# Attention values of one unit in four fed to TensorE in float32, and the splits of the rest moved to ScalarE and GpSimd

## The reference

```
x = x + 0.5 * ffn(layernorm(x))        # shared SwiGLU of width 704, plus top 2 of 8 experts of width 352
x = x + attention(layernorm(x))        # 16 query heads, 4 key/value heads, head size 32, rotary, no mask
x = x + 0.5 * ffn(layernorm(x))        # the same weights again
```

## Time and profile before

| | us |
|---|---|
| median of 3 runs | 1815.87 (1813.20 to 1818.67) |
| profiled execution | 1809.72 |
| its span | 1807.7 |
| TensorE busy | 1684.5 (93%) |
| VectorE busy | 1078.8 (60%) |
| ScalarE busy | 864.4 (48%) |
| GpSimd busy | 974.3 (54%) |
| mean granted clock of TensorE | 0.974 |

### The profile page before, as it was taken

How to read it: one execution, slowest core, us unless ns; L and a number is a source line. 1 busy time by engine, 2 the same in 40 slices (tenths; PEclk the granted TensorE clock), 3 DMA queues, 4 the chain that set the end, 5 groups by cost and what they waited for, 6 DMA issues and landing times.

```text
span 1807.7 us, 25091 instructions
## 1 busy us (share of the span) xinstructions
PE 1684.5 (93%) x8596; PEld 1344.3 (74%) x8596; DVE 1078.8 (60%) x1846; ACT 864.4 (48%) x1274; POOL 974.3 (54%) x727
## 2 busy tenths in 40 slices
PE   6999999999977989999999999877799999999997
PEld 5888898999866756666666666545688889999985
DVE  4554322222687879999999999995445432222226
ACT  4322232322324359999999998872323122322320
POOL 3115673336522148989898988840030619550745
PEclk9999999999988989999999999998989999999999
DMA  9205543333630000000000000003010535432427
GB/s 333 97 24 218 207 175 131 120 132 120 193 134 1 1 2 1 1 2 1 1 1 2 1 1 2 13 13 142 1 53 1 222 122 196 161 140 84 167 86 240
DMA packets 54310, 160.01 MB, mean 89 GB/s; under 512 B 6704, under 2 KB 7600, under 8 KB 51632
## 3 DMA queue, kind: packets, MB, share of 16 engines
q1 hardware_dynamic: 41360, 84.74, 13.3%
q0 software_dynamic: 12832, 73.67, 11.4%
HBM read 102.29 MB, written 55.84 MB: 87 GB/s over the span
## 4 chain that ended last, share of the span: by engine, by line
PE 60%; DVE 15%; ACT 12%; issue 6%; DMA 6%; POOL 1%; SPq 0%; ACTq 0%; POOLq 0%; DVEq 0%
PE PS L1021 11%; PE PS L1023 10%; PE PS L1022 10%; ACT PT L1487 5%; DVE nmf L1799 4%; PE PS L1217 4%; DMA xn<-x_routed 3%; ACT Ph L1494 3%; DMA xs<-x_routed 2%; PE PS L1143 2%; PE PS L1148 2%; PE PS L1146 2%; PE PS L1145 2%; PE PS L1147 2%; PE PS L1144 2%
## 5 line engine op out<-in xcount | busy, mean ns | idle before, releaser
L1956 POOL TENSOR_TENSOR Pl<-PT,Ph 128x1024 fp32r<-128x1024 f32 x176 | 433.4, 2475 | 86.4 <-ACT Ph L1494 81.4
L1799 DVE TENSOR_REDUCE nmf<-PS 128x1 f32<-128x1024 f32 x256 | 307.8, 1213 | 30.6 <-PE PS L1217 30.4
L1487 ACT ACTIVATE PT<-PS 128x1024 f32<-128x1024 f32 x256 | 259.5, 1014 | 23.7 <-PE PS L1235 17.0
L1250 PE MATMUL PS<-Ph,V 128*65 128x512 f32 x512 | 205.5, 401 | 13.5 <-DVE Pl L1822 12.7
L1494 ACT ACTIVATE Ph<-PT 128x1024 fp32r<-128x1024 f32 x184 | 194.9, 1059 | 35.0 <-PE PS L1251 32.6
L1251 PE MATMUL PS<-Pl,V 128*65 128x512 f32 x512 | 202.1, 395 | 0.0
L1871 POOL TENSOR_TENSOR W<-raw,W 128x544 fp32r<-128x544 f32 x144 | 190.1, 1355 | 1.5
L1217 PE MATMUL PS<-KS,QS 96*128 96x512 f32 x512 | 171.5, 416 | 19.0 <-ACT PT L1487 13.2
L1774 DVE TENSOR_TENSOR thid<-thid,PS 128x352 f32<-128x352 f32 x78 | 40.7, 521 | 245.8 <-ACT thid L1413 245.8
L1235 PE MATMUL PS<-QS,KS 98*128 98x512 f32 x512 | 173.2, 420 | 3.0 <-DVE nmf L1799 2.9
L1413 ACT ACTIVATE thid<-PS 128x352 f32<-128x352 f32 x78 | 36.2, 464 | 260.4 <-PE PS L1148 260.4
(11 more groups left out here) (183 smaller groups left out, 4107.9 us busy)
## 6 DMA issues: line engine op xcount, KB each, us to landing
raw<-ffn_w POOLq DMA_DIRECT2D x18, 2176.0 KB, 10.2
y_routed<-ytile SPq DMA_DIRECT2D x78, 256.0 KB, 2.1
xn<-x_routed SPq DMA_DIRECT2D x40, 256.0 KB, 2.8
x_routed<-xq SPq DMA_DIRECT2D x1, 9984.0 KB, 28.5
xs<-x_routed SPq DMA_DIRECT2D x38, 256.0 KB, 4.0
raw<-ffn_w SPq DMA_DIRECT2D x6, 768.0 KB, 10.6
raw<-ffn_w SPq DMA_DIRECT2D x2, 2176.0 KB, 9.2
x_home<-X SPq DMA_DIRECT2D x4, 1024.0 KB, 5.8
```

The lines of the kernel that those rows point to most:

```text
L1250: e.matmul(PS[0:VCOL, ob, :], V[:, b * QT + kt, g, :], Ph[:, u % PBUF, js], start=kt == 0, stop=False)
L1487: e.activation(PT[:, u % PTBUF, :], PS[:, i:i + 2, :].rearrange("p b n -> p (b n)"), ACT.Exp, scale=SCALE).then_inc(p_ready.sem, 1)
L1799: e.tensor_reduce(nmf[:, (n % 3) * REP + h, t:t + 1], PS[:, i:i + 2, :].rearrange("p b n -> p (b n)"), AX.X, ALU.max, negate=True).then_in ...
L1956: e.tensor_tensor(Pl[:, u % PBUF, :], PT[:, u % PTBUF, :], Ph[:, u % PBUF, :], ALU.subtract).then_inc(pl_pool.sem, 1)
```

## The change

- Units for which in_full(u) holds (u % 4 == 3, but not u % 16 == 15 outside group 7) are not split. Their values are two matmuls of V and PT, both read as plain float32, FULL_LAG = 3 units after their scores.
- All other units are split with Ph on ScalarE and Pl on GpSimd; only in group 7 does VectorE make Pl, for u % 4 == 1. VectorE makes no Ph.
- LAG is 5. Where the unit whose values are due is not the first of its half head and a next group exists, its values are issued in two halves: one key tile between scores and row_max, one behind row_max.
- A full unit's values come before the third unit's, so a half head ends with unit 2 of four where unit 3 is full (ends_half), else with unit 3.
- The copy to OT moves from ScalarE to VectorE, as does the copy of turned queries for the groups from 2 on.
- Buffers: 4 of PT, 6 of Ph, 5 of Pl, some of them in the place that Wo, MT, rL and head had; Wo and woraw move, and the first Wo load waits for the values of group 3.
- At the end of the loop, the values still due are issued as the split ones, then the full unit 255, then 254.

```diff
-PTBUF = 4
-PBUF = 4
-LAG = 4
+PTBUF, PHBUF, PLBUF = 4, 6, 5
+LAG, FULL_LAG = 5, 3
...
-def hi_on_vector(u):
-    return u % 4 == 1 or u // UNITS == len(KV_GROUPS) - 1 and u % 4 == 3
+def in_full(u):
+
+    return u % 4 == 3 and (u // UNITS == len(KV_GROUPS) - 1 or u % 16 != 15)
 
 
 def lo_on_vector(u):
-    return u % 4 == 2 or u // UNITS == len(KV_GROUPS) - 1 and u % 4 != 0
+    return u // UNITS == len(KV_GROUPS) - 1 and u % 4 == 1
+
+
+def ends_half(u):
+
+    return in_full(u + 1) if u % 4 == 2 else u % 4 == 3 and not in_full(u)
...
         work.append(("scores", u))
-        in_flight.append(u)
         if lows:
             work.append(("place_low", *lows.pop(0)))
+        w = u - LAG if u >= LAG and not in_full(u - LAG) else None
+
+        between = w is not None and unit(w)[3] > 0 and n + 1 < groups
+        if between:
+            work.append(("half_values", w, 0))
         if n + 1 < groups:
             work.append(("row_max", n + 1, un // QT, un % QT))
...
+        if w is not None:
+            work.append(("half_values", w, 1) if between else ("values", w))
+            if ends_half(w):
                 outputs.append(unit(w)[:3])
+        if u >= FULL_LAG and in_full(u - FULL_LAG):
+            work.append(("values", u - FULL_LAG))
...
+    end = groups * UNITS
+    assert in_full(end - 1) and LAG > FULL_LAG
+    for w in [v for v in range(end - LAG, end - 2) if not in_full(v)] + [end - 1, end - 2]:
         work.append(("values", w))
...
                 if c == 0:
+
                     sp.wait_ge(q_done, PROJECTED[-1])
-                    sp.wait_ge(max_turned, 0, REP - 1)
+                    sp.wait_ge(pv_done, NKV * UNITS - 1)
...
+            for j in tiles:
                 kt = 2 * pair + j
                 js = slice(j * GRP, (j + 1) * GRP)
-                e.matmul(PS[0:VCOL, ob, :], V[:, b * QT + kt, g, :], Ph[:, u % PBUF, js], start=kt == 0, stop=False)
-                mm = e.matmul(PS[0:VCOL, ob, :], V[:, b * QT + kt, g, :], Pl[:, u % PBUF, js],
-                              start=False, stop=kt == QT - 1)
-            mm.then_inc(pv_done.sem, 1)
-            free[ob] = (ot_ready, n, h, hf)
+                end = ends_half(u) and j == 1
+                if in_full(u):
+                    mm = e.matmul(PS[0:VCOL, ob, :], V[:, b * QT + kt, g, :].bitcast(F32), PT[:, u % PTBUF, js],
+                                  start=False, stop=end)
+                else:
+                    e.matmul(PS[0:VCOL, ob, :], V[:, b * QT + kt, g, :], high_part(u)[:, js],
+                             start=kt == 0, stop=False)
+                    mm = e.matmul(PS[0:VCOL, ob, :], V[:, b * QT + kt, g, :], low_part(u)[:, js],
+                                  start=False, stop=end)
+            if 1 in tiles:
+                mm.then_inc(pv_done.sem, 1)
+                free[ob] = (ot_ready, n, h, hf)
...
-                if u >= PTBUF:
-                    act.wait_ge(pl_dve if lo_on_vector(u - PTBUF) else pl_pool, u - PTBUF)
+                if u >= PTBUF and in_full(u - PTBUF):
+                    act.wait_ge(pv_done, u - PTBUF)
+                elif u >= PTBUF:
+                    parts_ready(act, u - PTBUF)
...
+            elif kind in VALUES and is_whole(key) and ends_half(key[0]):
...
+                dve.wait_ge(pv_done, u)
+                if i >= 1:
+                    dve.wait_ge(ot_turned, *heads[i - 1])
+                e.tensor_copy(OT[0:VCOL, :], PS[0:VCOL, out_bank(n, hf), :]).then_inc(ot_ready.sem, 1)
+            elif kind == "turn" and beside_heads(key[0]):
+                n, t = key
+                dve.wait_ge(stack_turned, n, t)
+                e.tensor_copy(QS[n % 3][0:STK, :, t * P:(t + 1) * P],
+                              PS[0:STK, MISC, :].rearrange("p (h n) -> p h n", n=P)).then_inc(stack_ready.sem, 1)
```

More of the change, by code:

```diff
@@ L412, in order_of_work @@
             maxima.append((n + 1, un // QT))
[L413 to L418, removed]
+        if in_parts and lo_on_vector(u - 1):
+            work.append(("split_lo", u - 1))
+        if w is not None:
+            work.append(("half_values", w, 1) if between else ("values", w))
+            if ends_half(w):
                 outputs.append(unit(w)[:3])
+        if u >= FULL_LAG and in_full(u - FULL_LAG):
+            work.append(("values", u - FULL_LAG))
         if outputs and pair == 1:
@@ L428, in order_of_work @@
             work.append(("wo", un // QT))
[L429 to L432, removed]
+    end = groups * UNITS
+    assert in_full(end - 1) and LAG > FULL_LAG
+    for w in [v for v in range(end - LAG, end - 2) if not in_full(v)] + [end - 1, end - 2]:
         work.append(("values", w))
-        if unit(w)[3] == QT // 2 - 1:
-            outputs.append(unit(w)[:3])
+        if outputs:
+            work.append(("store_head", *outputs.pop(0)))
+    outputs.append(unit(end - 2)[:3])
     work.append(("store_head", *outputs.pop(0)))
@@ L584, in macaron @@
     assert at <= g_at[LATE] + group_bytes
-    MT, at = place("MT", (QT, 2, 2, P), F32, wqkv_at)
+    assert ORDER[0] * TPG // QT == 1
+    Wo, at = place("Wo", (P, 2, DC, D), F32R, wqkv_at - NT // 2 * NKV * VCOL * 4)
+    woraw, _ = place("woraw", (P, D), F32, arena + NT * D * 4 + NKV * S * 4)
+    MT, at = place("MT", (QT, 2, 2, P), F32, at)
     rL, at = place("rL", (P, 2, TPG), F32, at)
     head, at = place("head", (P, 2, TPG, HD), F32, at)
-    Wo, at = place("Wo", (P, 2, DC, D), F32R, at)
-    woraw, at = place("woraw", (P, D), F32, at)
+    parts_at = [x_at + i * 2 * GRP * 4 for i in range(8)]
+    while len(parts_at) < PHBUF + PLBUF:
+        parts_at.append(at)
+        at += 2 * GRP * 4
     assert at <= wqkv_at + 2 * DC * QKV * 4
+    parts = [place(f"Ph{i}", (P, 2 * GRP), F32R, parts_at[i])[0] for i in range(PHBUF)]
+    parts += [place(f"Pl{i}", (P, 2 * GRP), F32R, parts_at[PHBUF + i])[0] for i in range(PLBUF)]
     PS = ctx.enter_context(nc.psum_tensor("PS", [P, 8, GRP], F32))
@@ L814, in macaron @@
         elif kind == "split_hi":
-            (ph_dve if hi_on_vector(*key) else ph_act).plan(*key)
+            ph_act.plan(*key)
         elif kind == "split_lo":
             (pl_dve if lo_on_vector(*key) else pl_pool).plan(*key)
[L818 to L821, removed]
+        elif kind in VALUES and is_whole(key):
+            u = key[0]
+            pv_done.plan(u)
+            if ends_half(u):
+                ot_ready.plan(*unit(u)[:3])
         elif kind == "store_head":
@@ L878, in is_projected_after, with parts_ready, high_part, low_part @@
         return PROJECTED.index(t) >= n
+    def parts_ready(lane, u):
+        if in_full(u):
+            lane.wait_ge(p_ready, u)
+        else:
+            lane.wait_ge(pl_dve if lo_on_vector(u) else pl_pool, u)
+    def high_part(u):
+        return parts[u % PHBUF]
+    def low_part(u):
+        return parts[PHBUF + u % PLBUF]
     def turned_halves(t):
@@ L893, in macaron @@
     head_place = {key: i for i, key in enumerate(heads)}
-    ends = [tuple(unit(key[0])[:3]) for kind, *key in work if kind == "values" and unit(key[0])[3] == QT // 2 - 1]
+    ends = [tuple(unit(key[0])[:3]) for kind, *key in work
+            if kind in VALUES and is_whole(key) and ends_half(key[0])]
     end_place = {key: i for i, key in enumerate(ends)}
@@ L1238, in scores, with values @@
             free[i] = free[i + 1] = (p_ready, u)
-        def values(u):
+        def values(u, *tiles):
             n, h, hf, pair = unit(u)
@@ L1327, in tensor_program @@
             elif kind == "values":
+                values(*key, 0, 1)
+            elif kind == "half_values":
                 values(*key)
@@ L1461, in scalar_program @@
                              src.unsqueeze(2).broadcast_to([P, REP, 2, HD]), ACT.Copy).then_inc(stack_hi.sem, 1)
-            elif kind == "turn":
+            elif kind == "turn" and not beside_heads(key[0]):
                 n, t = key
@@ L1484, in scalar_program @@
                 act.wait_ge(s_done, u)
-                if u >= PTBUF:
-                    act.wait_ge(pl_dve if lo_on_vector(u - PTBUF) else pl_pool, u - PTBUF)
+                if u >= PTBUF and in_full(u - PTBUF):
+                    act.wait_ge(pv_done, u - PTBUF)
+                elif u >= PTBUF:
+                    parts_ready(act, u - PTBUF)
                 e.activation(PT[:, u % PTBUF, :], PS[:, i:i + 2, :].rearrange("p b n -> p (b n)"),
                              ACT.Exp, scale=SCALE).then_inc(p_ready.sem, 1)
-            elif kind == "split_hi" and not hi_on_vector(*key):
+            elif kind == "split_hi":
                 u, = key
                 act.wait_ge(p_ready, u)
[L1492 to L1502, removed]
+                if u >= PHBUF:
+                    act.wait_ge(pv_done, u - PHBUF)
+                e.activation(high_part(u)[:], PT[:, u % PTBUF, :], ACT.Copy).then_inc(ph_act.sem, 1)
             elif kind == "attention_end":
```

53 lines of the change are left out of this document (26 added, 27 removed).

## The result

The changed kernel takes 1824.7 us (median of 4 runs, 1824.2 to 1825.5) against 1814.6 us of the kernel before on the same chip: ratio 1.0064, interval 1.0046 to 1.0081. It is 0.6% slower. The forecast was 1824.5.

A forecast was written before the change was run, and what follows sets the result against it. TensorE was to replace VectorE as the bound: 35.7 us of work plus 1.65 of waits made a 37.3 us period against 35.91. Terms +17, +1.4 and -9.7 gave +9 us, a 1824.5 us median, range 1796 to 1838.

The forecast's parts named there:

- The bound: Groups 0 to 6: TensorE sets the pace after the change, 35.7 us of work for 16 units; VectorE set it before.
- Float32, 0.91 a matmul and 1.83 a unit: Full units' values on TensorE: two float32 matmuls replace four float32r ones of 0.93 us in all, +0.9 us a unit.
- my column price: TensorE matmul price from spacings: 0.00044 us a column plus 0.004 fixed; four passes of 512 columns give 0.91 us.
- The waits, 0.35 three times and 0.6 once: 1.65: TensorE, per 16 units: 0.35 us for ScalarE's exponential three times, 0.6 for VectorE's OT copy once; period 37.3.
- Group 7, 7.1 a half head: Group 7's unit loop: 7.1 us a half head against 8.36, saving 9.7 us over 7.75 half heads.
- GpSimd at 34.4: GpSimd's work in 16 units: 13 low parts of about 2.37 us and four stacked parts of 0.91, beneath TensorE's period.
- Rival 1: TensorE's waits vanish through VectorE's slack and deeper lags: 35.9 us steady, -11 us, 1805 us; chance 0.22.
- Rivals 2, 3 and 4: Float32 matmul price: 2 cheaper, 1789 us; 3 dearer at 1.05, 1837 us, 0.10; 4 run as float32r; 2 and 4 0.20.
- The whole: Entire kernel: +17 us steady groups, +1.4 group 6, -9.7 group 7, +9 us in sum; median 1824.5 us.

The follow-up runs named there:

- the three edits of the order: Changed kernel with first unit's values also in halves, values ending a split half head ahead of the maxima, place_max behind values: period 35.31 us, ratio 0.991.
- group 7 alone: Changed kernel with full units only in group 7, older engine split and value order in groups 0 to 6, new buffers and LAG 5 kept: ratio 0.995.
- section 6: Changed kernel, reordered, without float32 in groups 0 to 6; VectorE makes the third unit's low part, GpSimd the fourth's: period 35.69 us, ratio 0.993.
- the first run without float32: Changed kernel with float32 only in group 7; elsewhere the fourth unit is split, low part on VectorE, in the change's order: period 41.0 us, ratio 1.035.
- the second: Changed kernel without float32 in groups 0 to 6, fourth unit's low part on VectorE, with values and place_max reordered: period 44.8 us, ratio 1.056.

## Why the prediction was right

*The bound.* TensorE sets the pace after, as said. One pass in place of float32 shows it, since the period falls with TensorE's work, and the three edits of the order show it again, since TensorE is then never idle and the period is its work. That VectorE set the pace before is read from its trace alone (34.2 us of work in 35.91); no run tests it.

*Float32, 0.91 a matmul and 1.83 a unit.* Measured 0.86 and 1.72, in two records of 0.43 each. It was 6% less than my column price. By the Trainium skill ("FP8 and Floating Point Precision", TensorE Precision Notes) true float32 is 4 passes; four times 512 columns in 0.86 us are 0.42 ns a column, one column a cycle at the 2.4 GHz level, so the trace agrees. The halved rate that the Trainium skill has for FP32_LOW_HIGH ("Perfetto Trace Analysis", Engine Utilization) would have given 0.46, by an estimate from the 0.23 of a float32r matmul, and is not what this matmul runs at. The term was 0.3 us too high in 16 units.

*The waits, 0.35 three times and 0.6 once: 1.65.* Measured 0.34 three times and 0.76 once, 1.78; by the period less that of the run without waits, 37.44 - 35.31, they are 2.1. The places and the count were right, and each was taken away by an edit at that place. The working of the 0.35 adds 0.75 and 1.03 to 1.84, where they make 1.78. The trace after has 1.82, from the scores at 883.17 to the maxima at 884.99: the exponential ends at 884.93, and the 0.06 behind it, for which the working named no row, is real. The OT copy takes 0.68 us, not 0.6. The half values were said to cover the other steps; with the halves undone the period is the same within 0.07 us, so there was little to cover. The place that I left out is the maxima's transpose, whose wait I had priced as nothing; it shows once the first unit's wait is covered, and is not shown to be the 0.3 us that is left here. Too little here and too much for float32 nearly cancel: 37.3 forecast, 37.44 measured.

*Group 7, 7.1 a half head.* Measured 7.02. The saving was more a half head than forecast, 9.3 us in six where 6 x 1.26 is 7.6, of which 1.1 to 1.5 is the clock in the kernel before. The two last half heads, which the forecast counted in, give back 1.2: together -8.1 against -9.7.

*GpSimd at 34.4* was wrong, for an edit that the sum did not need: low parts take 2.39 (2.42 before), but stacked parts 0.46 in place of 0.91. Its work is 32.9 us, and the room under TensorE's is 2.5 us, not 1.3. So its share was 86% (302.7 of 352 us) and not the 92% that I gave as a sign; VectorE's was 74%, near the 75% forecast.

*Rival 1, vanishing waits,* did not happen on its own, but its period is real: 35.31 once three items are reordered. The argument against it, that the wait is latency and order and not VectorE's load, is what the edits show. *Rivals 2, 3 and 4* are excluded by the 0.86 us a matmul, which is neither 0.23 nor 0.46 nor 1.05.

*The whole.* The forecast was +9 and the profiled executions differ by +14.6, 12.6 of it in the loop: every term there came out 0.2 to 2.1 us above its forecast. The median of before is 1814.6 with one more run, 1815.9 when I forecast +9; the ratio puts the difference at +8 to +15 us, so that the medians meet within 0.2 us is partly luck. The 2.1 us behind the loop, where the code is the same, can't be told from the spread: there the 14 traces take from 576.7 to 591.1 us.

## What to carry to other kernels

When a full engine is relieved by giving work to another, sum the receiver's work by the spacing of its starts, before any wait: here 35.4 us stood against a period of 35.9, so the most that groups 0 to 5 could gain was 0.5 us in 16 units, and four waits of 1.8 us in all ate it. Then look in the receiver's in-order queue for the steps left thin by the move; a few items set ahead of or behind a neighbour were worth 2.1 us a period, more than the 0.5 that the move could gain. Moving a share of work between engines (a float32 unit in none, two or three of four half heads) changes who waits for whom in each queue, and the time did not follow the sums: 35.69, 37.02, 35.31.

## What the runs showed of the hardware

- A float32 matmul of 128 x 65 weights and 512 columns leaves two matmul records and takes 0.86 us, 3.7 times a float32r one (0.232).
- VectorE and GpSimd held each other up, which I had priced as VectorE's own work. The high part on VectorE took 1.62 us on average, but in group 7 of the kernel before 0.67 to 0.69 where no GpSimd operation had begun ahead of it, and 2.88 where a low part had begun 0.8 us ahead, as these rows show:

```profile
1176.94 3.12 POOL L1956 TENSOR_TENSOR Pl<-PT,Ph 128x1024 fp32r<-128x1024 f32 x1 [2.07 <-ACT Ph L1494]
...
1177.74 2.88 DVE L1816 CAST Ph<-PT 128x1024 fp32r<-128x1024 f32 x1
...
1182.72 0.69 DVE L1816 CAST Ph<-PT 128x1024 fp32r<-128x1024 f32 x1
```

- GpSimd's stacked part fell from 0.91 to 0.46 us with VectorE's high parts gone, and with them restored (group 7 alone) it was back; with only a low part restored on VectorE (the third unit's, in section 6) it stayed at 0.46. The rows of the run with group 7 alone, columns as above:

```profile
L1881 DVE CAST Ph<-PT 128x1024 fp32r<-128x1024 f32 x39 | 60.8, 1560 | 0.0
...
L2008 POOL TENSOR_TENSOR TS<-qtok,TS 128x128 fp32r<-128x128 f32 x39 | 35.4, 909 | 0.0
```

- Where two low parts met, the one that began first was served first. In the first run without float32 VectorE's began 0.12 us ahead: 1.22 us on VectorE and 3.34 on GpSimd. In the second GpSimd's began 0.98 us ahead: 2.41 on GpSimd and 2.51 on VectorE. The Trainium skill ("SBUF — State Buffer", Who interferes with whom) says that the two engines share a port pair under an exclusive lock; these numbers agree.
- A copy of 512 columns from PSUM took 0.68 us on VectorE and 0.58 on ScalarE.
